# A chunked scan's attention products moved from GpSimd to VectorE, with C·B read from PSUM and the residual sum put last in the loop

## The chip, the cores and the metric

One core of a Trainium2 chip (trn2). The metric is the device time of the whole program in microseconds (us). A NeuronCore has five engines with a queue each, which meet through semaphores: TensorE (PE; its weight loads are PEld), VectorE (DVE), ScalarE (ACT), GpSimd (POOL) and SyncE (SP), which here issues the DMAs. Matmul results land in eight banks of PSUM; everything else is in SBUF.

## The reference

`x` is 16 images of 192 channels, 32 by 32 pixels, float32. Two blocks run on each image, each with a group norm ahead and a residual sum behind:

```
x = x + L0(_gn(x))      # in-projection, 3x3 depthwise convolution, silu, chunked scan, layer norm, gate, out-projection
x = x + L1(_gn(x))      # projection, selective scan with 16 states per channel, out-projection
```

The chunked scan of L0 goes over 1024 tokens in 8 chunks of 128, with 12 heads of 32 channels and a state of 32. For a chunk it is

```
att = einsum('bcihn,bcjhn->bcijh', Ch, Bh) * Lmat * dtc      # Lmat = exp(cumsum_i - cumsum_j), causal
y_intra = einsum('bcijh,bcjhp->bcihp', att, xc)
y_inter = Ch . exp(cumsum) . state before the chunk
state = state * exp(whole chunk's sum) + B . decay . x
y = layer_norm(y_intra + y_inter + D x) * z, then the out-projection
```

C·B, the first product of `att`, is the same for the 12 heads: it is one 128x128 matrix for a chunk.

## The kernel before, in words

A pass handles two images at once: the selective scan of L1 for image b, and all of L0 (with the first part of L1) for image b+1. There is a first pass with L0 alone (image 0), a last one with the end of L1 alone, and a loop over two passes in the middle. Each pass is cut into 48 slots. The order on each engine is the order of the code: every engine has a function `run` that walks the slots `s` and calls, in a slot, the parts of both images. The engines are tied by semaphores only (`wait_ge` and `then_inc`).

**L1's selective scan.** One unit per slot, 48 units of 128x512. ScalarE makes the decay (L955: `dec`, or `bank`), VectorE makes the input `wr` (L1234) and runs the scan into `hst` (L1247), GpSimd multiplies by C into `hc` (L754), and TensorE sums two units' `hc` with `sel` every even slot (L1284, `bank<-hc,sel`). In a slot VectorE does scan and `wr` after its parts of `first_block_soon` and ahead of `first_block_later`.

**L0's chunked scan.** `chunk_at(s, stage)` says which chunk c is at a stage: slot s = 14 + 2c + stage. A chunk takes two slots per step, and up to five chunks are under way at once. In slots of stage 0, 2, 4, 6, 8 ("even") and 1, 3, 5, 7, 9 ("odd"):

- stage 0: TensorE: `b_by_c` (C·B into bank 4, `B_CBT`, columns 0 to 127; in the trace `bank<-cs_,bs`), the first group of `rows` (L1368: four heads' cumulative sums spread over 128 rows), `transposed_x` (L1382, L1383).
- stage 1: TensorE: `from_state` (`bank<-state,cs_`, in front of it the wait for the state), `rows` 1, later in the slot `rows` 2. ScalarE: the exponentials of group 0 (L831, into `att`), the copy of x to `xtok` (L875), the copy of C·B to the SBUF tile `cbt` (L879). GpSimd: `scaled_x` (L701), then `attention` for heads 0 to 3 (L710: `att` times `cbt`, which is repeated for each head).
- stage 2: ScalarE: the exponentials of groups 1 and 2 (L831). GpSimd: `attention` for heads 4 to 11 (L710). TensorE: `own_state`. VectorE: `from_state` (L1088).
- stage 3: TensorE: `chunk_output`, first with `diagd`, then 12 matmuls of 128x32 that read `att`. VectorE: `carry_state` (L1082, L1083: the state times its decay, plus the bank).
- stage 4: VectorE: `chunk_output` (L1102, L1099 for the first chunk: the sum of y; L1105 to L1108: its statistics). GpSimd: `layer_rstd` (L715).
- stage 5: VectorE: `normalise` (L1112). TensorE: `transposed_y` into bank 4, columns 128 to 511 (L1430).
- stage 6: ScalarE: the bank copy to `yzt` with weight and bias of the norm (L861). TensorE: `gate`.
- stage 7: VectorE: `gate` (L1119: `yzt` times the gate's bank).
- stage 8: TensorE: `projected` (`bank<-ssd,wo`).
- stage 9: VectorE: `residual` (L1125, L1126).

All tiles of L0's scan (`att`, `xtok`, `xw`, `yint`, `y0`, `yzt`) are parts of one SBUF tensor named `ssd` in the trace. `att` and `cbt` have two copies each, for even and odd chunks. VectorE's order inside an odd slot is residual, state, norm, gate, scan, `wr`; inside an even slot it is `from_state`, sum of y with statistics, scan, `wr`. The helper `mm` puts most matmuls on L1284.

## Time and profile before

| | us |
|---|---|
| median of three runs | 4015.2 |
| the three runs | 4018.0, 3992.5, 4015.2 |
| the profiled execution | 3989.6 |
| its span, first to last instruction | 3987.8 |
| mean granted clock of TensorE | 0.89 of full speed |
| distance from one image to the next in the middle of the run | about 241 |

The distance between images is read from GpSimd's rows: the same product of two images starts at 2000.35 and 2241.76 us. Busy time and rows are of the profiled execution. A row gives an instruction's start and duration; in brackets stands how long its engine had been idle, and whose end released it. TensorE's rows overlap, since matmuls are pipelined.

### The profile page before, as it was taken

Reading aid. Unit: us, or ns where it says so; the run is one execution under the profiler, and the core shown is the slowest. Engines: PE = TensorE matmul, PEld = TensorE weight load, DVE = VectorE, ACT = ScalarE, POOL = GpSimd, SP = SyncE. Lnnn points to the kernel's source line nnn. Section 1 sums busy time; section 2 is a strip of 40 time slices with the busy share of each in tenths; the row PEclk is TensorE's granted clock in tenths of the full one; section 3 lists DMA queues with packets and bytes.
Section 4 is the critical chain, followed back from the end, with each engine's and each line's share of the span. In section 5 each row is a group of like instructions: output and inputs, shape, how many; then the busy total and the mean of one; then the engine's idle time right before and its main releaser. Section 6 shows DMA issues by size and latency. Waiting matters only on the chain. (4 is left out here: it accounts for less than half of the span.)

```text
span 3987.8 us, 62307 instructions
## 1 busy us (share of the span) xinstructions
PE 3274.6 (82%) x20256; PEld 1864.8 (47%) x20256; DVE 2674.3 (67%) x3855; ACT 1844.2 (46%) x4475; POOL 2035.9 (51%) x1363
## 2 busy tenths in 40 slices
PE   4778888887987978888887897978888888888875
PEld 2645446363453635436363463635536354463620
DVE  1346857678585776757678575775757668575798
ACT  1425454363544536444463534535454353544542
POOL 1325546364453745546365463745546364563755
PEclk8989989898998989989898998989989898998986
DMA  3032131312213132130422213132131312313122
GB/s 64 1 94 68 68 86 34 112 62 79 81 40 112 51 107 74 67 82 33 120 62 78 81 40 112 51 106 69 48 108 33 118 63 74 82 45 101 62 73 77
DMA packets 104179, 291.11 MB, mean 73 GB/s; under 512 B 25373, under 2 KB 27020, under 8 KB 103820
## 3 DMA queue, kind: packets, MB, share of 16 engines
q1 hardware_dynamic: 103820, 286.71, 23.8%
q8 instruction: 179, 2.93, 0.3%
q14 instruction: 180, 1.47, 0.1%
HBM read 181.84 MB, written 39.85 MB: 56 GB/s over the span
## 5 line engine op out<-in xcount | busy, mean ns | idle before, releaser
L754 POOL TENSOR_TENSOR hc<-hst,bcrep 128x512 f32<-128x512 f32 x768 | 1187.6, 1546 | 1227.8 <-DVE hst L1247 1199.8
L710 POOL TENSOR_TENSOR ssd<-ssd,cbt 128x512 f32<-128x512 f32 (+1 forms) x256 | 585.4, 2287 | 383.8 <-ACT ssd L831 364.2
L1234 DVE TENSOR_TENSOR wr<-durep,bcrep 128x512 f32<-128x512 f32 x768 | 644.4, 839 | 65.1 <-DMA bcrep<-bc_rows 65.1
L1284 PE MATMUL bank<-hc,sel 128*32 128x512 f32 x1536 | 474.6, 701 | 104.2 <-POOL hc L754 104.2
L955 ACT ACTIVATE bank<-durep,aneg 128x512 f32<-128x512 f32 x368 | 252.0, 690 | 514.0 <-DVE hst L1247 468.5
L831 ACT ACTIVATE ssd<-bank,ncs 128x128 f32<-128x128 f32 x1536 | 432.8, 401 | 74.6 <-PE bank L1284 72.5
L1284 PE MATMUL bank<-ssd 128*128 128x32 f32 (+1 forms) x3296 | 448.0, 288 | 7.4 <-POOL ssd L710 7.4
L1247 DVE TENSOR_TENSOR_SCAN hst<-dec,wr 128x512 f32<-128x512 f32 x256 | 358.2, 1399 | 135.6 <-ACT dec L955 63.0
L1284 PEld LDWEIGHTS bank<-ssd 128*128 128x128 f32 x3296 | 397.8, 193 | 15.1 <-POOL ssd L710 10.8
L1284 PE MATMUL bank<-xna,wt0a 128*128 128x128 f32 (+3 forms) x1088 | 320.1, 398 | 76.2 <-DVE xnb L1065 76.2
L861 ACT ACTIVATE ssd<-bank,nbc,nwc 128x128 f32<-128x128 f32 x384 | 147.8, 454 | 498.8 <-PE bank L1430 498.5
L1284 PE MATMUL bank<-ssd,wcv 64*32 64x512 f32 x5376 | 344.1, 591 | 0.0
L1247 DVE TENSOR_TENSOR_SCAN hst<-bank,carry,wr 128x512 f32<-128x512 f32 x240 | 306.9, 1279 | 29.4 <-issue 11.2
L955 ACT ACTIVATE dec<-durep,aneg 128x512 f32<-128x512 f32 x400 | 294.1, 740 | 7.1 <-DVE hst L1247 4.6
L1284 PE MATMUL bank<-xnb,wt0b 128*128 128x128 f32 (+3 forms) x1088 | 295.3, 374 | 0.0
L1284 PEld LDWEIGHTS bank<-xna,wt0a 128*128 128x128 f32 (+1 forms) x1088 | 183.1, 203 | 232.3 <-issue 195.5
L1368 PE MATMUL bank<-ident,csum 128*128 128x128 f32 x1536 | 257.3, 294 | 30.6 <-ACT ssd L831 30.6
L1368 PEld LDWEIGHTS bank<-ident,csum 128*128 128x128 f32 x1536 | 196.2, 149 | 89.4 <-ACT ssd L831 49.6
L1125 DVE TENSOR_TENSOR x1a<-bank,xa 128x128 f32<-128x128 f32 x128 | 37.1, 290 | 285.7 <-PE bank L1284 285.7
L1284 PEld LDWEIGHTS bank<-xnb,wt0b 128*128 128x128 f32 (+1 forms) x1088 | 178.7, 201 | 76.6 <-issue 76.6
L1247 DVE TENSOR_TENSOR_SCAN hst<-dec,carry,wr 128x512 f32<-128x512 f32 x144 | 209.2, 1453 | 6.9 <-issue 2.8
L1284 PE MATMUL bank<-ssd,wo 128*128 128x128 f32 (+1 forms) x1536 | 211.9, 280 | 1.2 <-DVE ssd L1119 1.0
(188 smaller groups left out, 5022.5 us busy)
## 6 DMA issues: line engine op xcount, KB each, us to landing
durep<-scratch SPq DMA_DIRECT2D x192, 512.0 KB, 3.8
bcrep<-bc_rows SPq DMA_DIRECT2D x128, 512.0 KB, 5.5
ssd<-stage SPq DMA_DIRECT2D x384, 140.4 KB, 2.9
ssd<-bcst SPq DMA_DIRECT2D x128, 74.4 KB, 2.1
xa<-in_x_dram SPq DMA_DIRECT2D x16, 512.0 KB, 5.3
scratch<-u SPq DMA_DIRECT2D x32, 256.0 KB, 2.0
scratch<-delta SPq DMA_DIRECT2D x32, 256.0 KB, 2.2
out_dram<-x1a SPq DMA_DIRECT2D x16, 512.0 KB, 5.1
```

The costliest lines, as they stand in the source:

```text
L710: nc.gpsimd.tensor_tensor(a, a, bc(cbt[:, c % 2, :].unsqueeze(1), [P, h1 - h0, Q]), ALU.mult).then_inc(att_ready.sem, 1)
L754: nc.gpsimd.tensor_tensor(hc[:, i % CRING, :], hst[:, i % HRING, :], bcrep[:, g, 1, :], ALU.mult).then_inc(hc_ready.sem, 1)
L831: ins = nc.scalar.activation(att[:, c % 2, h, :], bank[ROW_BANKS[r]][:, k * Q:(k + 1) * Q], ACT.Exp, bias=ncs[:, c, h:h + 1])
L861: ins = nc.scalar.activation(yzt[:, c % 2, m, :], bank[B_CBT][:, (m + 1) * Q:(m + 2) * Q], ACT.Identity, bias=nbc[:, m:m + 1], scale=nwc[: ...
L955: nc.scalar.activation(decay_of(i), durep[:, j % SLOTS_DU, 0, :], ACT.Exp, scale=aneg1[:, g * NB + k:g * NB + k + 1]).then_inc(decay_ready ...
L1125: nc.vector.tensor_tensor(x1a[par][:, t], bank[B_OUT][:, 0:Q], xa[:, t], ALU.add).then_inc(x1_ready.sem, 1)
L1234: nc.vector.tensor_tensor(wr[:, i % WRING, :], durep[:, j % SLOTS_DU, 1, :], bcrep[:, g, 0, :], ALU.mult).then_inc(w_made.sem, 1)
L1247: nc.vector.tensor_tensor_scan(hst[:, i % HRING, :], decay_of(i), wr[:, i % WRING, :], carry[:, g:g + 1] if hf else 0.0, ALU.mult, ALU.add ...
L1284: return nc.tensor.matmul(out, lhsT, rhs, start=start, stop=stop, skip_group_check=True)
L1368: nc.tensor.matmul(ps[:, k * Q:(k + 1) * Q], bc(csum[:, 0, c, h:h + 1], [P, P]), ident[:, :], start=(k == 0), stop=False, is_transpose=Tru ...
```

## The change

- The attention products are made by VectorE in one instruction for all 12 heads (1536 elements), reading C·B from bank 4 as it is; it stands at the end of the even slot (stage 2), in `first_block_later`. GpSimd's two products and ScalarE's copy to `cbt` go, and with them the tile and its semaphore.
- `b_by_c` moves from stage 0 to stage 2, ahead of the `rows` in the same even slot. Since bank 4 is shared, it waits for the products of the chunk before and for the bank copy of the chunk two before; `transposed_y` waits for the products too.
- ScalarE does the exponentials of group 1 ahead of the bank copy of stage 6, and those of group 2 behind it.
- VectorE's residual sum moves from the head of the odd slot to its end, behind scan and `wr`.

```diff
-            def attention(n, c, h0, h1):
-
-                pool.wait_ge(row_exp.sem, row_exp.at(n, NRB * c + h1 // HPB))
-                pool.wait_ge(cbt_copied.sem, cbt_copied.at(n, c + 1))
-                a = att[:, c % 2, h0:h1, :]
-                nc.gpsimd.tensor_tensor(a, a, bc(cbt[:, c % 2, :].unsqueeze(1), [P, h1 - h0, Q]),
-                                        ALU.mult).then_inc(att_ready.sem, 1)
...
-                    attention(n, c, 0, HPB)
-                c = chunk_at(s, 2)
-                if c >= 0:
-                    attention(n, c, HPB, NH)
...
+                c = chunk_at(s, 2)
+                if c >= 0:
+                    exp_rows(n, c, 1)
                 c = chunk_at(s, 6)
...
                 c = chunk_at(s, 2)
                 if c >= 0:
-                    exp_rows(n, c, 1)
                     exp_rows(n, c, 2)
...
-                    act.wait_ge(cb_ps.sem, cb_ps.at(n, c + 1))
-                    if c >= 2:
-                        act.wait_ge(att_ready.sem, att_ready.at(n, 2 * (c - 1)))
-                    nc.scalar.copy(cbt[:, c % 2, :], bank[B_CBT][:, 0:Q]).then_inc(cbt_copied.sem, 1)
...
+            def attention(n, c):
+
+                dve.wait_ge(row_exp.sem, row_exp.at(n, NRB * (c + 1)))
+                dve.wait_ge(cb_ps.sem, cb_ps.at(n, c + 1))
+                a = att[:, c % 2, :, :]
+                nc.vector.tensor_tensor(a, a, bc(bank[B_CBT][:, 0:Q].unsqueeze(1), [P, NH, Q]), ALU.mult).then_inc(att_ready.sem, 1)
...
-                c = chunk_at(s, 9)
-                if c >= 0:
-                    if c == 0 and again:
-
-                        dve.wait_ge(stored.sem, stored.at(n - 2, 32))
-                    residual(n, c, par)
                 c = chunk_at(s, 3)
...
+                c = chunk_at(s, 2)
+                if c >= 0:
+                    attention(n, c)
                 c = chunk_at(s, SSD_LAST)
+                if c >= 0:
+                    if c == 0 and again:
+
+                        dve.wait_ge(stored.sem, stored.at(n - 2, 32))
+                    residual(n, c, par)
...
                 if c >= 1:
-                    pe.wait_ge(cbt_copied.sem, cbt_copied.at(n, c))
-                if c >= 3:
-
-                    pe.wait_ge(yt_made.sem, yt_made.at(n, c - 2))
+                    pe.wait_ge(att_ready.sem, att_ready.at(n, c))
+                if c >= 2:
+
+                    pe.wait_ge(yt_made.sem, yt_made.at(n, c - 1))
                 mm(bank[B_CBT][:, 0:Q], bs[:, t], cs_[:, t], True, True).then_inc(cb_ps.sem, 1)
...
-                if c + 2 < NCH:
-                    pe.wait_ge(cbt_copied.sem, cbt_copied.at(n, c + 3))
-                else:
+                if c + 1 < NCH:
+                    pe.wait_ge(att_ready.sem, att_ready.at(n, c + 2))
+                if c >= 1:
                     pe.wait_ge(yt_made.sem, yt_made.at(n, c))
...
+                c = chunk_at(s, 2)
+                if c >= 0:
+                    b_by_c(n, c)
                 c = chunk_at(s, 0)
                 if c >= 0:
...
-                    b_by_c(n, c)
```

The order on VectorE in a chunk with all stages under way, before: from scan and `wr` of an even slot (L1247, L1234) through the odd slot to the sum of y (`x1a`, `x1b` are the residual, `state` the state, `ssd` L1112 the norm, L1119 the gate):

```order
L1234 TENSOR_TENSOR wr<-durep,bcrep 128x512 [waits scanned]
L1125 TENSOR_TENSOR x1a<-bank,xa 128x128 [waits o0_ps]
L1126 TENSOR_TENSOR x1b<-bank,xb 64x128
L1082 TENSOR_TENSOR state<-state,cexp 32x384 [waits state_ps]
L1083 TENSOR_TENSOR state<-state,bank 32x384 [waits dve_steps]
L1112 TENSOR_SCALAR ssd<-ssd,lmv,lrs 128x384 [waits lrs_ready]
L1119 TENSOR_TENSOR ssd<-ssd,bank 128x384 [waits z_ps,yt_made]
L1247 SCALAR_TENSOR_TENSOR hst<-dec,wr 128x512 [waits hc_ready,carried,w_made,decay_ready]
L1234 TENSOR_TENSOR wr<-durep,bcrep 128x512 [waits scanned]
L1088 TENSOR_TENSOR ssd<-bank,cexp 128x384 [waits inter_ps]
L1102 TENSOR_TENSOR ssd<-ssd,bank 128x384 [waits yint_ready,yt_ps,y_ps]
```

The same place now (`ssd` L1104 of 128x1536 is the attention product; the lines of the code have shifted):

```order
L1227 TENSOR_TENSOR wr<-durep,bcrep 128x512 [waits scanned]
L1104 TENSOR_TENSOR ssd<-ssd,bank 128x1536 [waits cb_ps,row_exp]
L1066 TENSOR_TENSOR state<-state,cexp 32x384 [waits state_ps]
L1067 TENSOR_TENSOR state<-state,bank 32x384 [waits dve_steps]
L1096 TENSOR_SCALAR ssd<-ssd,lmv,lrs 128x384 [waits lrs_ready]
L1110 TENSOR_TENSOR ssd<-ssd,bank 128x384 [waits z_ps,yt_made]
L1240 SCALAR_TENSOR_TENSOR hst<-dec,wr 128x512 [waits hc_ready,carried,w_made,decay_ready]
L1227 TENSOR_TENSOR wr<-durep,bcrep 128x512 [waits scanned]
L1116 TENSOR_TENSOR x1a<-bank,xa 128x128 [waits o0_ps]
L1117 TENSOR_TENSOR x1b<-bank,xb 64x128
L1072 TENSOR_TENSOR ssd<-bank,cexp 128x384 [waits inter_ps]
L1086 TENSOR_TENSOR ssd<-ssd,bank 128x384 [waits yint_ready,yt_ps,y_ps]
```

The product is new ahead of the state update; the residual, with its wait for the projection (`o0_ps`), went from ahead of the state update to behind `wr`.

The order on ScalarE in an even slot of such a chunk, before (L955 is the decay, L861 the bank copy, L831 the exponentials, four heads each):

```order
L955 ACTIVATE dec<-durep,aneg 128x512 [waits scanned,du_read0]
L861 ACTIVATE ssd<-bank,nbc,nwc 128x128 [waits o0_ps,yt_ps]
L861 ACTIVATE ssd<-bank,nbc,nwc 128x128 x2
L831 ACTIVATE ssd<-bank,ncs 128x128 [waits row_ps]
L831 ACTIVATE ssd<-bank,ncs 128x128 x3
L831 ACTIVATE ssd<-bank,ncs 128x128 [waits row_ps]
L831 ACTIVATE ssd<-bank,ncs 128x128 x3
```

And now (L939 is the decay, L817 the exponentials, L850 the bank copy):

```order
L939 ACTIVATE dec<-durep,aneg 128x512 [waits scanned,du_read0]
L817 ACTIVATE ssd<-bank,ncs 128x128 [waits row_ps]
L817 ACTIVATE ssd<-bank,ncs 128x128 x3
L850 ACTIVATE ssd<-bank,nbc,nwc 128x128 [waits o0_ps,yt_ps]
L850 ACTIVATE ssd<-bank,nbc,nwc 128x128 x2
L817 ACTIVATE ssd<-bank,ncs 128x128 [waits row_ps]
L817 ACTIVATE ssd<-bank,ncs 128x128 x3
```

One group of exponentials passed the bank copy, the other stayed behind it.

## Rows read from the trace of the kernel before

**Rows 1.** The page, busy time of the engines (share of the span), count

```profile
PE 3274.6 (82%) x20256; PEld 1864.8 (47%) x20256; DVE 2674.3 (67%) x3855; ACT 1844.2 (46%) x4475; POOL 2035.9 (51%) x1363
```

**Rows 2.** Stretches: us; busy PE, PEld, DVE, ACT, POOL; clock; DMA share, GB/s

```profile
2019.13:2030.79 11.66, 9.65 (x61) 6.76 (x62) 10.52 (x13) 8.53 (x25) 11.57 (x8) 1.00 0.06 25
2030.79:2042.70 11.91, 10.50 (x74) 8.26 (x74) 10.66 (x14) 8.96 (x25) 8.59 (x7) 1.00 0.16 45
2042.70:2056.37 13.67, 12.15 (x87) 9.62 (x87) 9.99 (x17) 6.54 (x22) 10.23 (x8) 1.00 0.14 40
...
2083.71:2097.52 13.81, 12.79 (x89) 9.97 (x89) 9.36 (x17) 5.98 (x20) 9.30 (x7) 1.00 0.00 1
```

**Rows 3.** Timeline of PE in one full chunk: start, us, instruction, idle before

```profile
2070.04 0.91 PE L1284 MATMUL bank<-state,cs_ 128*128 128x384 f32 x2 [1.29 <-DVE state L1083]
...
2076.80 0.49 PE L1284 MATMUL bank<-cs_,bs 128*128 128x128 f32 x2
...
2077.52 0.65 PE L1368 MATMUL bank<-ident,csum 128*128 128x128 f32 x4 [0.23 <-ACT ssd L831]
```

**Rows 4.** Timeline of DVE in the same chunk

```profile
2068.20 0.29 DVE L1125 TENSOR_TENSOR x1a<-bank,xa 128x128 f32<-128x128 f32 x1 [3.47 <-PE bank L1284]
...
2068.60 0.81 DVE L1082 TENSOR_TENSOR state<-state,cexp 32x384 f32<-32x384 f32 x1
2069.44 0.54 DVE L1083 TENSOR_TENSOR state<-state,bank 32x384 f32<-32x384 f32 x1
...
2070.75 0.54 DVE L1119 TENSOR_TENSOR ssd<-ssd,bank 128x384 f32<-128x384 f32 x1
...
2072.41 1.68 DVE L1234 TENSOR_TENSOR wr<-durep,bcrep 128x512 f32<-128x512 f32 x1
...
2074.91 0.56 DVE L1102 TENSOR_TENSOR ssd<-ssd,bank 128x384 f32<-128x384 f32 x1 [0.35 <-PE bank L1284]
...
2077.87 0.67 DVE L1234 TENSOR_TENSOR wr<-durep,bcrep 128x512 f32<-128x512 f32 x1
```

**Rows 5.** Waits: engine, line, whom it waited for: us, times, longest

```profile
PE bank L1284 <- DVE state L1083: 124.5, 94, 2.7
```

**Rows 6.** Groups by shape, the products on GpSimd: busy us, mean ns

```profile
L710 POOL TENSOR_TENSOR ssd<-ssd,cbt 128x1024 f32<-128x1024 f32 x128 | 314.3, 2455 | 364.5 <-ACT ssd L831 364.2
...
L710 POOL TENSOR_TENSOR ssd<-ssd,cbt 128x512 f32<-128x512 f32 x128 | 271.2, 2118 | 19.3 <-ACT cbt L879 19.3
```

**Rows 7.** Timeline of POOL in the same chunk

```profile
2070.58 2.97 POOL L710 TENSOR_TENSOR ssd<-ssd,cbt 128x512 f32<-128x512 f32 x1
```

**Rows 8.** Timeline around the second `state` matmul of the image

```profile
2026.83 2.79 DVE L1234 TENSOR_TENSOR wr<-durep,bcrep 128x512 f32<-128x512 f32 x1
...
2029.54 0.54 DVE L1082 TENSOR_TENSOR state<-state,cexp 32x384 f32<-32x384 f32 x1
...
2030.79 0.88 PE L1284 MATMUL bank<-state,cs_ 128*128 128x384 f32 x2 [2.02 <-DVE state L1083]
```

**Rows 9.** Groups by shape on DVE: busy us, mean ns, idle before

```profile
L1247 DVE TENSOR_TENSOR_SCAN hst<-bank,wr 128x512 f32<-128x512 f32 x128 | 156.1, 1219 | 56.8 <-ACT bank L955 53.1 <-issue 2.5
...
L1119 DVE TENSOR_TENSOR ssd<-ssd,bank 128x384 f32<-128x384 f32 x128 | 68.7, 537 | 0.0
...
L1125 DVE TENSOR_TENSOR x1a<-bank,xa 128x128 f32<-128x128 f32 x128 | 37.1, 290 | 285.7 <-PE bank L1284 285.7
```

**Rows 10.** Timeline of ACT in the same chunk: the bank copy

```profile
2075.28 1.16 ACT L861 ACTIVATE ssd<-bank,nbc,nwc 128x128 f32<-128x128 f32 x3 [4.90 <-PE bank L1430]
```

**Rows 11.** Timeline of the tail: the last chunks' output and norm

```profile
2108.47 2.87 PE L1284 MATMUL bank<-ssd 128*128 128x32 f32 x24 [0.25 <-POOL ssd L710]
...
2108.94 1.41 DVE L1112 TENSOR_SCALAR ssd<-ssd,lmv,lrs 128x384 f32<-128x384 f32 x1 [1.07 <-POOL lrs L715]
...
2118.22 0.55 PE L1430 MATMUL bank<-ident,ssd 128*128 128x128 f32 x3 [0.96 <-DVE ssd L1112]
```

**Rows 12.** Group on PE, the head rows' wait: busy us, mean ns, idle before

```profile
L1368 PE MATMUL bank<-ident,csum 128*128 128x128 f32 x1536 | 257.3, 294 | 30.6 <-ACT ssd L831 30.6
```

More of the change, by code:

```diff
@@ L249, in build @@
         wend = sb("wend", [P, NCH, NH])
-        cbt = sb("cbt", [P, 2, Q])
         state = sb("state", [P, DI])
@@ L343, in build @@
         cb_ps = sig("cb_ps", NCH)
-        cbt_copied = sig("cbt_copied", NCH)
         row_ps = sig("row_ps", NCH * NRB)
         row_exp = sig("row_exp", NCH * NRB)
-        att_ready = sig("att_ready", 2 * NCH)
+        att_ready = sig("att_ready", NCH)
         xw_ready = sig("xw_ready", NCH - 1)
@@ L1415, in chunk_output @@
                     mm(bank[B_XY][:, m * P:(m + 1) * P], xs[m][:, t], diagd[:, m, :], m == 0, False)
-                pe.wait_ge(att_ready.sem, att_ready.at(n, 2 * (c + 1)))
+                pe.wait_ge(att_ready.sem, att_ready.at(n, c + 1))
                 for h in range(NH):
```

## The prediction

> **What bounds the kernel now.** I read the page first, then the stretches between two fixed points, then the waits, then four engines' rows of one chunk. TensorE is the busiest engine by far: 3274.6 us of a span of 3987.8, against 2674.3 for VectorE and 2035.9 for GpSimd [rows 1]. That is a mean and decides nothing, so I looked at the scan over chunks of one image (slots 14 to 37) in the middle of the run. Its fixed points are the starts of the matmul that reads `state` in front of chunks 1 to 7. The six distances are 11.66, 11.91, 13.67, 13.67, 13.67 and 13.81 us, and TensorE is busy for 9.65, 10.50, 12.15, 12.15, 12.16 and 12.79 of them [rows 2] (the first three and the last; the two between read as the third). So 1.0 to 2.0 us of each chunk is TensorE idle, at a granted clock of 1.00.
>
> What ends that idle time stands in the chunk's rows. After the transposes of x TensorE waits 1.29 us, until VectorE's update of the state ends (2069.44 + 0.54); another 0.23 us it waits for ScalarE's exponentials [rows 3]. The rows of VectorE say why the update is late: VectorE sat idle for 3.47 us in front of the residual sum at 2068.20, which needs the output projection, the last work of TensorE before those transposes. Residual and state update stand in one queue, so the update (0.81 and 0.54 us) starts only when the projection is through, though its own input was there 3 us before [rows 4]. The wait table confirms this for the whole run: 124.5 us in 94 waits for that one instruction [rows 5].
>
> GpSimd is the second cause, and it rules the early chunks. It spends 271.2 + 314.3 us on the products that the change takes away [rows 6]. While one runs, a VectorE product of two SBUF tiles waits for its end: at 2072.41 `wr` took 1.68 us beside GpSimd's 2.97 us product (from 2070.58), and ended 0.5 us after it; at 2077.87, with GpSimd idle, it took 0.67 [rows 4, 7]. At 2026.83 it took 2.79 us, just ahead of a state update that TensorE waited 2.02 us for [rows 8].
>
> **The change, part by part.** It moves no DMA and nothing in the queues of SyncE.
>
> Residual last. The state update no longer stands behind the projection. In a full chunk (chunks 3 to 6) that ends the 1.29 us wait, if nothing else of VectorE is as late; that is the sum over the new chain below.
>
> The product on VectorE. One instruction of 1536 elements, one operand in PSUM. The trace has no such size. The nearest rows are the product of an SBUF tile with a PSUM bank: 128x384 in 537 ns, the sum of the same kind 128x128 in 290 ns [rows 9]. That is 0.965 ns per element and 0.166 us fixed: 0.166 + 1536 x 0.965 ns = 1.65 us, the value I take. Below it there is little: 1536 elements at that slope alone are 1.48 us. Above it, the slowest VectorE form near by is the scan, 1219 ns for 512 elements [rows 9], thus 2.38 ns per element and 3.66 us; with a wait for a GpSimd product of 1.27 us on top, 4.93 us.
>
> Whether it waits for GpSimd matters. Product and gate share one form (SBUF times PSUM), and the gate at 2070.75 began inside GpSimd's product and still took 0.54 us [rows 4, 7]; all 128 of them have a mean of 537 ns. So no wait, 1.65 us. The Trainium skill says the same from the other side (GPSIMD Engine Reference, Key points): GpSimd contends with VectorE instructions that have two SBUF inputs or run in a two-port mode. By that rule `wr` waits and the new product doesn't, and the trace agrees (1.68 against 0.54). The skill also has a rule that speaks against reading PSUM (VectorE: DVE Perf Modes, the TRN2 errata): a PSUM source costs 120 cycles fixed and an SBUF one 58. By it the product would be an estimated 1656 cycles at 0.96 GHz, 1.73 us. That makes the two chunks below that VectorE sets 0.08 us longer and the others not at all, some 2.5 us in the run.
>
> The new chain on VectorE. From the state update's end to TensorE's matmul 0.06 us; from that matmul (2070.04) to the sum of y (2074.91) 4.87; from there through statistics, scan and `wr` to 2078.54, 3.63; the new product 1.65; the update, without GpSimd beside it 0.54 + 0.54 with gaps, 1.11 [rows 3, 4, 8]. Sum 11.3 us per chunk. What the product waits for is there by then: in full chunks ScalarE's last exponentials now follow the bank copy (2075.28 + 1.16 + some 1.1 = 2077.6) and C·B ends at 2077.3, both ahead of 2078.54 [rows 10, 3]. Queued behind the product are the state update and all of the odd slot, and TensorE waits for the update; that is in the chain.
>
> Which is longer, chunk by chunk. Distances 1 and 2: chain 11.3 against TensorE's 9.65 and 10.50; the chain sets the pace: 11.66 + 11.91 - 2 x 11.3 = 1.0 us. Distances 3 to 5: TensorE's 12.15 is longer, 3 x (13.67 - 12.15) = 4.6 us. Distance 6: 13.81 - 12.79 = 1.0. Together 6.6 us.
>
> The exponentials moved. The second group runs in ScalarE's 4.90 us of idle time instead of behind it [rows 10]; that ends the 0.23 us wait, already in the 12.15. The copy of C·B (0.27 us on ScalarE) goes; ScalarE is idle beside it: nothing.
>
> C·B two steps later. As many matmuls per slot; it now waits for the bank copy (end 2076.44), which is 0.36 us before TensorE comes to it anyway, at 2076.80 [rows 3, 10]. Only the last one is extra, in a slot that had none: +0.42 us, its 0.49 less the overlap with the next. In the first image TensorE has no units of the other scan to sum ahead of it, and the wait shows, some 0.5 us per chunk (my estimate from the same two rows).
>
> The tail (chunk 7's output). A wait of 0.25 us for GpSimd's product goes and one of 0.96 us for the norm, which stood behind a residual [rows 11]; 0.25 + 0.96 - 0.42 = 0.8. The norm after it waited 1.07 us for a power that GpSimd did behind its product [rows 11]; I count half. Tail: 1.3 us.
>
> Sum: 6.6 + 1.3 = 7.9 us in each of 15 images, 119; the first image 7.9 less 6 x 0.5 and the early chunks, some 6. 125 us in all. The profiled execution took 3989.6 us (span 3987.8 and 1.8 around it): 3865. The runs' median lies 0.6% above it, their fastest at 3992.5, so a run may come out anywhere from 3865 to 3890; I name 3875.
>
> **Rivals.**
>
> B, the port: the product waits for GpSimd's product in progress, 1.27 us more. For it: every SBUF-SBUF form does so. Against: the gate doesn't. Chain 11.3 + 1.27 = 12.6: the early pair loses 1.6 us, the full chunks gain 3 x 1.1, the last 1.0, the tail 0.8: 3.5 us (3 x 1.1 + 1.0 + 0.8 - 1.6) x 16 = 56, 3935.
>
> C, slower: the product is priced above the point where the new chain outlasts the old distances. The six distances are 78.4 us, with the tail's 0.8 they are 79.2, and the chain is 9.67 + p: 79.2 / 6 = 13.2, so p = 3.5 us. At 4.93 us (rate of the scan plus the wait) the chain is 14.6, six of them 87.6, 8.4 us lost per image: 3990 + 16 x 8.4 = 4125. For it: only the scan's row. Against: three rows of the nearer form.
>
> D, no gain: the wait is only exchanged. The product comes ahead of the state update and needs all three groups of exponentials; if they or the rate put it at 3.5 us behind `wr` in place of 1.65, the point above is met: 3990. For it: the copy waits for TensorE's transposes, one chain more. Against: 0.9 us of slack at 2078.54.
>
> E, more: the early chunks too fall to TensorE's time, and in the tail VectorE's gain carries into the next stage; TensorE's two waits of the chunks go in all (124.5 and 30.6 us) [rows 5, 12] and the tail's 1.3 x 16 = 21 with them: 176 us, 3814, or somewhat less, up to 3830.
>
> **How the numbers follow.** Chances: forecast 0.68 (own range 3835 to 3910), B 0.12, C 0.04, D 0.06, E 0.10. The range reaches from E's edge to B with the runs' 0.6% on it: 3818 to 3955. Over 1% faster (1% is about what a measurement tells from no change; 3950 or less): forecast, E and most of B, 0.87. Within 1%: D and some of B and C, 0.09. Slower 0.04.
>
> **What would show it.** Right: 128 VectorE products near 1.65 us; the `state` matmuls 12.2 us apart in full chunks and 11.3 in the first; TensorE's wait for the state update near zero in full chunks and 1 to 2 us in the two early ones; `wr` near 0.7 us throughout; the residual without idle time ahead. Wrong: a product over 2.5 us, or distances still over 13; a new wait of TensorE for the product or for the bank copy; a product that lasts longer where GpSimd works.

## The result, and the profile after

The changed kernel takes 3838.6 us (median of four runs, 3832.4 to 3840.1), against 4003.9 us for the kernel before in the same session (3992.4 to 4018.0). The ratio is 0.958, 95% interval 0.954 to 0.963. A second session of five runs gave 3843.3 us against 3990.9, ratio 0.962 (0.960 to 0.964). The forecast was 3875 us in a range of 3818 to 3955; the measured 3838.6 is 36 us below the 3875 and inside the range. The profiled execution of after took 3839.4 us with a span of 3837.7, at a mean granted clock of 0.89 as before, so the profiled executions lie 150 us apart where 125 were forecast. One run of all that follow was slow, e2's second (9435 us at a granted clock of 0.33), and e2's median leaves it out.

The page of after, busy time of the engines, beside [rows 1]:

```profile
PE 3214.6 (84%) x20256; PEld 1841.5 (48%) x20256; DVE 2655.5 (69%) x3983; ACT 1829.5 (48%) x4347; POOL 1498.1 (39%) x1107
```

GpSimd is relieved of 538 us. VectorE, which took over the products (223.7 us), is busy for 19 us less than before: its other instructions got shorter by more than that, `wr` alone by 122 us. TensorE's busy time falls by 60 us with the same count of matmuls. Of that, 26 us stand in the distances 3 to 6 (783.5 to 757.8 us over all images, at a granted clock of 1.00 in both), which says that "busy" held something there that was no work; more on that below. Another 29 us stand in the convolution's stretch, where the clock isn't full, and are not explained by it.

The stretches between `state` matmuls of one image in the middle of the run, columns as in [rows 2] (the first, second, third, fourth and last distance; the one left out reads as the fourth):

```profile
1953.28:1964.81 11.53, 9.65 (x62) 6.78 (x62) 8.51 (x14) 7.86 (x23) 6.32 (x5) 1.00 0.07 21
1964.81:1975.89 11.08, 10.28 (x74) 8.23 (x74) 8.39 (x15) 8.54 (x24) 3.76 (x3) 1.00 0.08 30
1975.89:1987.66 11.77, 11.77 (x86) 9.66 (x87) 9.79 (x17) 5.74 (x19) 4.66 (x4) 1.00 0.12 46
1987.66:1999.34 11.68, 11.68 (x89) 9.58 (x87) 9.36 (x18) 6.26 (x20) 4.90 (x4) 1.00 0.41 143
...
2011.01:2023.54 12.53, 12.53 (x90) 9.95 (x89) 10.42 (x19) 6.26 (x18) 5.09 (x4) 1.00 0.00 1
```

From the third distance on TensorE has no idle time at all; the first two still hold 1.9 and 0.8 us of it. TensorE's rows of a full chunk, answering to [rows 3], show both old waits gone (more rows of before stand further down):

```profile
2005.99 0.49 PE L1277 MATMUL bank<-cs_,bs 128*128 128x128 f32 x2
2006.32 0.60 PE L1361 MATMUL bank<-ident,csum 128*128 128x128 f32 x4
2006.76 0.38 PE L1277 MATMUL bank<-maskneg,identb 128*128 128x512 bf16 x1
...
2010.90 0.27 PE L1376 MATMUL bank<-ident,bs 128*128 128x128 f32 x1
2011.01 0.81 PE L1277 MATMUL bank<-state,cs_ 128*128 128x384 f32 x2
2011.66 0.60 PE L1361 MATMUL bank<-ident,csum 128*128 128x128 f32 x4
```

VectorE's rows of the same chunk, answering to [rows 4]. The product stands right behind `wr`, the state update right behind the product, the residual behind the next `wr` with no idle time:

```profile
2007.07 0.67 DVE L1227 TENSOR_TENSOR wr<-durep,bcrep 128x512 f32<-128x512 f32 x1
2007.65 1.75 DVE L1104 TENSOR_TENSOR ssd<-ssd,bank 128x1536 f32<-128x1536 f32 x1
2009.31 0.54 DVE L1066 TENSOR_TENSOR state<-state,cexp 32x384 f32<-32x384 f32 x1
2009.89 0.54 DVE L1067 TENSOR_TENSOR state<-state,bank 32x384 f32<-32x384 f32 x1
...
2012.99 0.27 DVE L1116 TENSOR_TENSOR x1a<-bank,xa 128x128 f32<-128x128 f32 x1
```

The update ends at 2010.43, 0.58 us ahead of the matmul that reads it. The waits of the whole run, answering to [rows 5] and [rows 12]:

```profile
PE bank L1277 <- DVE state L1067: 42.7, 32, 2.7
PE bank L1361 <- ACT ssd L817: 22.4, 17, 1.5
PE bank L1277 <- DVE state L1064: 9.9, 16, 1.3
```

The wait for the state update fell from 124.5 us (94 times) to 42.7 (32 times, two per image). The wait for ScalarE's exponentials that is left (22.4 us of 30.6) stands ahead of the first `state` matmul, once per image, and not in the full chunks. The wait for the first chunk's copy of the state, 16 times 0.20 us before, has grown to 9.9 us. VectorE's groups by shape, beside [rows 9]. First `wr` in the kernel before, then after:

```profile
L1234 DVE TENSOR_TENSOR wr<-durep,bcrep 128x512 f32<-128x512 f32 x768 | 644.4, 839 | 65.1 <-DMA bcrep<-bc_rows 65.1
```

```profile
L1227 DVE TENSOR_TENSOR wr<-durep,bcrep 128x512 f32<-128x512 f32 x768 | 522.0, 680 | 47.0 <-DMA bcrep<-bc_rows 47.0
...
L1104 DVE TENSOR_TENSOR ssd<-ssd,bank 128x1536 f32<-128x1536 f32 x128 | 223.7, 1748 | 53.1 <-PE bank L1277 34.5 <-ACT ssd L817 18.6
...
L1116 DVE TENSOR_TENSOR x1a<-bank,xa 128x128 f32<-128x128 f32 x128 | 35.3, 276 | 2.9 <-PE bank L1277 2.7
```

`wr`, untouched by the change, is 0.16 us shorter as a mean. GpSimd's products are what made it long: in e6 below, the kernel before without them, its mean is 693 ns. The residual's idle time fell from 285.7 us to 2.9.

Where the time went, over all 16 images. The program is cut at the same instructions in both traces (start of the `csum` copy on VectorE, the seven `state` matmuls, the second instruction of the last residual, the next `csum` copy), and each distance summed:

| stretch | before | after | difference | forecast |
|---|---|---|---|---|
| `csum` to first `state` matmul | 328.5 | 338.3 | +9.8 | 0 |
| distances 1 and 2 | 382.3 | 359.4 | -22.9 | -16 |
| distances 3 to 5 | 654.9 | 561.2 | -93.8 | -74 |
| distance 6 | 220.7 | 199.4 | -21.3 | -16 |
| last `state` matmul to next `csum` | 2293.3 | 2271.6 | -21.7 | -21 |
| all, with the program's start | 3987.8 | 3837.7 | -150.1 | -125 |

(The forecast's 2 us less for the first image are in its last line only.)

Two lines of this table hold something besides the change, the granted clock. The first distance of before took 11.67 us in 12 of the 14 middle images (11.46 in one of them) and 14.20 in two, where the clock stood at 0.76:

```profile
1058.65:1072.85 14.20, 13.07 (x62) 8.86 (x62) 10.99 (x13) 7.09 (x23) 12.65 (x9) 0.76 0.16 65
```

After has no such image. The distances 3 to 6 stood at 1.00 in both kernels, so their lines are clean.

### The profile page after: what moved, and what is told of

It is laid out like the page before. It is cut to its first block and busy times, and to the rows that moved or that the text cites. A ratio compares the mean times of both kernels' runs of the same rounds, so it can differ in the third digit from the quotient of the medians.

```text
span 3837.7 us, 61535 instructions
## 1 busy us (share of the span) xinstructions
PE 3214.6 (84%) x20256; PEld 1841.5 (48%) x20256; DVE 2655.5 (69%) x3983; ACT 1829.5 (48%) x4347; POOL 1498.1 (39%) x1107
## 5 line engine op out<-in xcount | busy, mean ns | idle before, releaser
L1227 DVE TENSOR_TENSOR wr<-durep,bcrep 128x512 f32<-128x512 f32 x768 | 522.0, 680 | 47.0 <-DMA bcrep<-bc_rows 47.0
L1277 PE MATMUL bank<-hc,sel 128*32 128x512 f32 x1536 | 466.1, 690 | 102.9 <-POOL hc L740 101.3
L817 ACT ACTIVATE ssd<-bank,ncs 128x128 f32<-128x128 f32 x1536 | 440.4, 380 | 112.9 <-PE bank L1277 110.3
L939 ACT ACTIVATE bank<-durep,aneg 128x512 f32<-128x512 f32 x368 | 251.9, 689 | 504.6 <-DVE hst L1240 464.8
L1240 DVE TENSOR_TENSOR_SCAN hst<-dec,wr 128x512 f32<-128x512 f32 x256 | 341.3, 1333 | 141.4 <-ACT dec L939 98.3
L699 POOL TENSOR_TENSOR ssd<-ssd,wend 128x384 f32<-128x384 f32 x112 | 157.5, 1406 | 372.9 <-ACT ssd L863 372.3
L939 ACT ACTIVATE dec<-durep,aneg 128x512 f32<-128x512 f32 x400 | 290.5, 730 | 7.1 <-DVE hst L1240 4.6
L850 ACT ACTIVATE ssd<-bank,nbc,nwc 128x128 f32<-128x128 f32 x384 | 147.8, 454 | 302.9 <-PE bank L1423 302.9
L1104 DVE TENSOR_TENSOR ssd<-ssd,bank 128x1536 f32<-128x1536 f32 x128 | 223.7, 1748 | 53.1 <-PE bank L1277 34.5
L705 POOL TENSOR_TENSOR lrs<-lve,neghalf 128x1 f32<-128x1 f32 x128 | 75.5, 590 | 384.6 <-DVE lve L1092 381.7
```

Of the source, the lines that this page charges most:

```text
L699: nc.gpsimd.tensor_tensor(xw[:, c % 2, :].rearrange("p (h d) -> p h d", d=HD), xtok[:, c % 2, 0:DI].rearrange("p (h d) -> p h d", d=HD), b ...
L705: nc.gpsimd.tensor_tensor(lrs[:, c % 2:c % 2 + 1], lve[:, c % 2:c % 2 + 1], neghalf[:, 0:1], ALU.pow).then_inc(lrs_ready.sem, 1)
L817: ins = nc.scalar.activation(att[:, c % 2, h, :], bank[ROW_BANKS[r]][:, k * Q:(k + 1) * Q], ACT.Exp, bias=ncs[:, c, h:h + 1])
L850: ins = nc.scalar.activation(yzt[:, c % 2, m, :], bank[B_CBT][:, (m + 1) * Q:(m + 2) * Q], ACT.Identity, bias=nbc[:, m:m + 1], scale=nwc[: ...
L939: nc.scalar.activation(decay_of(i), durep[:, j % SLOTS_DU, 0, :], ACT.Exp, scale=aneg1[:, g * NB + k:g * NB + k + 1]).then_inc(decay_ready ...
L1104: nc.vector.tensor_tensor(a, a, bc(bank[B_CBT][:, 0:Q].unsqueeze(1), [P, NH, Q]), ALU.mult).then_inc(att_ready.sem, 1)
```

## The experiments

The runs were made in three sessions (e1 to e4; e5 to e8; e9 to e12); each ratio is against the kernel before of the same session. Below, "six distances" are those between `state` matmuls, as a mean over the 14 middle images, worked out from the matmuls' starts. For before they are 12.02, 11.91, 13.66, 13.67, 13.66, 13.82, and for after 11.52, 11.08, 11.77, 11.67, 11.67, 12.53: 78.7 and 70.2 us per image. A mean of the first two can hold images at a lower granted clock; where it does, the text says so.

**e1: the kernel before, with the residual last and nothing else.**

```diff
-                c = chunk_at(s, 9)
-                if c >= 0:
...
-                    residual(n, c, par)
                 c = chunk_at(s, 3)
...
                 c = chunk_at(s, SSD_LAST)
+                if c >= 0:
...
+                    residual(n, c, par)
```

> The kernel before with one edit: the residual sum goes behind scan and wr. Products stay on GpSimd. My theory (the state update stood behind the projection in VectorE's queue; that alone is the 1.3 us wait of full chunks): the distance between state matmuls in full chunks falls from 13.67 to about 12.1 us, the early two stay at 11.7 and 11.9, 6 us per image, about 3895 us for a run of 3990. Rival (GpSimd's products beside VectorE are what makes the update late): full chunks stay above 13.2 us, over 3960 us.

Measured: 3902.0 us (3896.8 to 3909.3), ratio 0.975 (0.972 to 0.977). The stretches of one image, first, second and a full chunk:

```profile
1986.10:1997.78 11.68, 9.65 (x62) 6.78 (x62) 10.12 (x13) 8.54 (x25) 11.18 (x8) 1.00 0.03 12
1997.78:2009.68 11.90, 10.50 (x75) 8.26 (x75) 10.66 (x14) 8.94 (x25) 8.59 (x7) 1.00 0.16 45
...
2021.89:2034.01 12.12, 11.89 (x88) 9.53 (x87) 11.78 (x17) 6.42 (x21) 9.07 (x7) 1.00 0.36 130
```

The full chunks fall from 13.67 to 12.12 with GpSimd's products still in place; the early ones don't move in this image. Over the run the first is longer as a mean (12.74), because six of the 14 images took 14.20 us at a granted clock of 0.76; the other eight took 11.67 (one of them 11.47), as before. So it is the queue behind the residual that held the full chunks, not GpSimd, and this part alone is worth 100 us. Of these the traces ascribe only the distances, 79 us, to it: the stretch from the last `state` matmul to the last residual grew from 30.05 to 32.92 us per image, and the convolution's behind it fell from 110.5 to 107.5. What of these two is the edit and what the clock isn't separated.

**e2: after, with the residual back at the head of the odd slot** (the diff of e1 backwards).

> The changed kernel with one edit undone: the residual sum is back at the head of the odd slot. My theory: TensorE's wait for the state update is back in full chunks, distance about 13.1 us (13.67 less 0.39 for the exponentials and 0.27 for a state product that no longer waits for GpSimd), early two as in the changed kernel (11.5 and 11.1), 5 to 6 us per image, about 3925 us. Rival (relief of GpSimd did it): full chunks under 12.2 us, about 3850.

Measured: 3906.2 us (3905.7 to 3909.6), ratio 0.977 (0.973 to 0.980). Six distances 11.52, 11.08, 13.02, 12.96, 12.96, 13.82. VectorE in a full chunk:

```profile
2025.53 1.75 DVE L1104 TENSOR_TENSOR ssd<-ssd,bank 128x1536 f32<-128x1536 f32 x1
2028.64 0.29 DVE L1116 TENSOR_TENSOR x1a<-bank,xa 128x128 f32<-128x128 f32 x1 [1.36 <-PE bank L1278]
```

The product is done early, the residual waits for the projection again and the state update behind it is late: TensorE waits for it for 109.1 us in the run. The early distances are exactly those of after, since no residual stands in them. Moving the products alone doesn't free the full chunks; moving the residual alone doesn't free the early ones.

**e6: the kernel before, with GpSimd's products cut to one column.** The attention products are left out (the output lacks them); waits and signals stay.

```diff
-                a = att[:, c % 2, h0:h1, :]
-                nc.gpsimd.tensor_tensor(a, a, bc(cbt[:, c % 2, :].unsqueeze(1), [P, h1 - h0, Q]),
+                a = att[:, c % 2, h0, 0:1]
+                nc.gpsimd.tensor_tensor(a, a, cbt[:, c % 2, 0:1],
```

> The kernel before with the products left out: GpSimd multiplies one column where it did 512 or 1024 elements, so the attention isn't scaled by C.B; queues, waits and order stay. It prices GpSimd's products as such. My theory: early distances fall by about 1 us each (to 10.5 and 10.9), full chunks only to 13.4 us, since the residual is still ahead of the state update; some 3 us per image, about 3945 us. Rival (GpSimd's contention is the main thing): full chunks under 12.5 us, under 3900 us.

Measured: 3886.7 us (3871.2 to 3898.9), ratio 0.972 (0.969 to 0.976). The first, second and a full distance of one image:

```profile
1968.38:1977.96 9.58, 9.58 (x61) 6.74 (x61) 6.56 (x13) 6.47 (x22) 6.03 (x6) 1.00 0.04 15
1977.96:1988.56 10.60, 10.37 (x75) 8.37 (x75) 8.26 (x14) 10.00 (x24) 6.01 (x7) 1.00 0.13 49
...
2001.93:2015.33 13.40, 12.15 (x86) 9.62 (x86) 8.30 (x17) 6.35 (x22) 6.04 (x7) 1.00 0.46 156
```

This is e1's mirror: full chunks stay at 13.4 us, while the early two fall to 9.58 and 10.60, TensorE's own time or nearly so (9.58 and 10.37 busy). The gain is well above the expectation's 3945, because three places gain and not two: 2.4 + 1.3 us in the early distances, 0.8 over the other four, and 2.1 in the stretch from the last `state` matmul to the last residual (30.05 to 27.97): 6.6 us per image, some 106 in the run. Some 1.2 us of the 6.6 is the clock, which stood below 1.00 in before: against its images at 1.00 (11.67 for the first distance, 29.18 from the last `state` matmul to the last residual) the gain is 5.4. GpSimd's products cost the early chunks and the tail more than the forecast had seen.

**e3 and e12: after, with ScalarE's order undone**, and **e9: e1 with ScalarE's order of the change added.** The edit of e3; e9 makes it the other way:

```diff
-                c = chunk_at(s, 2)
-                if c >= 0:
-                    exp_rows(n, c, 1)
                 c = chunk_at(s, 6)
...
                 if c >= 0:
+                    exp_rows(n, c, 1)
                     exp_rows(n, c, 2)
```

> The changed kernel with ScalarE's order undone: the exponentials of group 1 behind the bank copy again. My theory: TensorE waits for them again (0.23 us and the refill, 0.4 us) and the VectorE product gets its last group 1.1 us later, which its slack of 0.9 us nearly covers: full chunks 12.0 to 12.3 us against 11.67, some 2 us per image, about 3870 us. Rival (ScalarE has slack in any order): 3840, distance 11.67.

> The kernel before with two of the change's parts alone: residual sum last, and the exponentials of group 1 ahead of the bank copy; the products stay on GpSimd. With the residual alone (run e1) the full chunks took 12.1 to 12.2 us, the early two 12.74 and 11.92, the whole 3902. Theory: the full chunks fall to 11.7 us, since GpSimd's products set nothing there, and the early two stay at 12.7 and 11.9, since those are GpSimd's. If a microsecond of a chunk is a microsecond of the run, that is 3 x 0.45 x 16 = 22 us and some 3880. Rival, the gain comes back elsewhere: in the stage of the convolution, whose length goes with the granted clock, so that the run stays at 3900 while the chunks are shorter.

e9 measured 3862.2 us (3852.5 to 3870.3), ratio 0.968 (0.965 to 0.970), where e1 has 0.975: ScalarE's order is worth some 30 us there, taken across two sessions. Its full chunks took 11.7 us as after's do, with the products still on GpSimd. The early distances are shorter than e1's as well (12.20 and 11.57), which the theory hadn't expected. For the first that is only the clock: 11.67 us in the images at 1.00 as in e1, but three at 0.76 and not six. For the second it is real (11.90 to 11.55 at 1.00).

e3 measured 3835.8 us (3835.3 to 3843.9), ratio 0.959 (0.957 to 0.962), that is, no loss against after at all. Yet its full chunks took 12.12 us against 11.67. The expectation of a repeat, in one session with after:

> Run e3 once more (the changed kernel with the exponentials of group 1 behind the bank copy). Full chunks 12.1 us, 1.6 us more per image over the chunks. Theory, given back: the time is that of the changed kernel again, within 5 us, and the stage of the convolution some 1.5 to 2.3 us shorter per image (106.7 against 109.0 before), at a higher granted clock. Rival, chance: the equal times of the first pair were luck, and this one is 15 to 25 us slower than the changed kernel.

> The changed kernel once more, beside its version with ScalarE's order undone, so that the two have the same chip and the same minutes. 3839 within 8 us. In its profile the full chunks stay at 11.67 us; the stage of the convolution (109.0 us per image in the first profile) tells how far that one moves from one execution to another.

e12 measured 3837.7 us (3832.0 to 3841.7) and after again (e11) 3843.3 (3837.9 to 3846.4): not chance. The chunks of e12 are longer by 1.6 us per image (71.9 against 70.2), and it is not slower. What pays for that stands in the stretch behind the chunks, from the last residual to the next `csum` copy, where the convolution runs: 106.9 us as a mean in e12 and 106.7 in e3, against 109.0 in both profiles of after. The mean granted clock there was 0.85 in e12 and e3, and 0.83 and 0.84 in the two of after. The stretch of one image, after first and then e3:

```profile
2053.53:2160.80 107.27, 88.63 (x545) 34.63 (x546) 66.71 (x93) 40.89 (x78) 39.22 (x27) 0.86 0.37 111
```

```profile
2050.98:2153.57 102.59, 85.44 (x545) 33.05 (x546) 66.80 (x92) 40.80 (x78) 39.41 (x27) 0.87 0.39 116
```

The work is the same; TensorE's matmuls are busy for 3.2 us longer in after, at a lower granted clock. What makes this stage's clock differ between two kernels that differ only in the chunks isn't shown by any run.

**e10: e5 (below) with ScalarE's order undone**, to see whether this gift comes with the order itself.

> The kernel of run e5 (product behind the state update) with ScalarE's order undone: the exponentials of group 1 behind the bank copy again. The pair e5 and e10 repeats the pair after and e3 at a shorter distance in the early chunks. Theory: full chunks 12.1 us against 11.67, thus 22 us more in the chunks; if that reaches the end, 3784 + 22 = 3806. Rival, given back: the time stays within 8 us of 3784, and the stage of the convolution is shorter by some 1.5 us per image at a higher granted clock.

Measured: 3808.5 us (3800.2 to 3814.8), 24 us above e5's 3784.2 of another session; ratio 0.953 (0.951 to 0.956) against e5's 0.948, whose interval (0.944 to 0.952) just overlaps. Full chunks 12.11 us. Its stretch of the convolution is 108.0 us, e5's 107.5: no gift this time, and the 0.45 us per full chunk reach the end. So ScalarE's part is worth some 22 to 30 us in two of three pairs, both taken across sessions, and nothing in the kernel as changed.

**e4: after, with C·B read from an SBUF tile** that ScalarE copies from the bank.

```diff
+                    act.wait_ge(cb_ps.sem, cb_ps.at(n, c + 1))
+                    nc.scalar.copy(cbt[:, c % 2, :], bank[B_CBT][:, 0:Q]).then_inc(cbt_copied.sem, 1)
...
-                nc.vector.tensor_tensor(a, a, bc(bank[B_CBT][:, 0:Q].unsqueeze(1), [P, NH, Q]), ALU.mult)
+                nc.vector.tensor_tensor(a, a, bc(cbt[:, c % 2, :].unsqueeze(1), [P, NH, Q]), ALU.mult)
```

> The changed kernel with C.B copied to an SBUF tile by ScalarE (0.27 us, behind the last exponentials) and the VectorE product reading that tile: two SBUF operands. If a product of two SBUF operands waits for GpSimd's hc product, its mean is 1.7 plus up to 1.3 us, about 2.9, every chunk's distance is 12.5 to 12.8 us, about 3925 us. If reading PSUM is what costs (0.1 us over my 1.65), the product is shorter here, 1.6 to 1.7 us, and the time is that of the changed kernel, 3835 to 3845.

Measured: 3919.8 us (3917.8 to 3939.7), ratio 0.981 (0.978 to 0.985): half of the gain is gone. GpSimd and VectorE in a full chunk:

```profile
2044.03 1.63 POOL L742 TENSOR_TENSOR hc<-hst,bcrep 128x512 f32<-128x512 f32 x1 [0.81 <-DVE hst L1246]
```

```profile
2044.45 2.83 DVE L1110 TENSOR_TENSOR ssd<-ssd,cbt 128x1536 f32<-128x1536 f32 x1
```

With two SBUF operands the product takes 2.83 us beside `hc` and, at its shortest in the run, 1.74, which is what the PSUM form takes everywhere. `hc` had 1.21 us left when the product began (2044.03 + 1.63 - 2044.45); 2.83 less 1.21 is 1.62, so it waited for `hc`'s end and then ran. That holds over the run: 104 of the 128 products of e4 began inside an `hc` that had 0.06 to 1.22 us left, and each is as long as that rest and 1.61 to 1.70 us more; the 24 others took 1.74 to 1.76. In after the product at 2007.65 took 1.75, and all 128 lie between 1.739 and 1.756, most of them begun inside an `hc` too. The early distances, which VectorE's chain sets, grew to 12.64 and 13.83 as a mean. The second is 12.17 us in the images at a clock of 1.00, 1.1 us above after's 11.09 as the product's 2.83 is above 1.75; it is 13.82 at 0.88 and 15.5 at 0.67. So what the early chunks lose is the wait for `hc` and, as a mean, the clock. The copy has a small share: the product waited 61.3 us in the run for it, but 51 of these stand ahead of the first `state` matmul, in a stretch that is only 0.3 us per image longer than in after.

**e7: after, with the product cut to one column.** The attention product is left out.

> The changed kernel with the VectorE product left out (one column in place of 1536 elements, so the attention isn't scaled by C.B). It prices the product on VectorE's path. My theory: early distances fall by the product's 1.7 us until TensorE's own time stops them, to about 10.0 and 10.4 us, full chunks stay at 11.67 (slack), about 3800 us. Rival (VectorE's chain also sets the full chunks): they fall to about 10 us, under 3740 us.

Measured: 3780.1 us (3773.2 to 3789.3), ratio 0.944 (0.941 to 0.947). Six distances 10.64, 10.50, 11.77, 11.67, 11.67, 12.53. The full chunks don't change by 0.01 us: there the product's 1.7 us is free. The early ones do, by 1.5 us together: there VectorE is the bound. In the profiles, 50 us apart, these two distances give 24 us; another 21 stand in the convolution's stretch (107.4 us as a mean against 109.0), which the product doesn't touch.

**e5: after, with the product behind the state update** in the odd slot, in place of at the end of the even one.

```diff
                 if 0 <= c < NCH - 1:
                     carry_state(n, c, step)
+                if c >= 0:
+                    attention(n, c)
...
-                c = chunk_at(s, 2)
-                if c >= 0:
-                    attention(n, c)
```

> The changed kernel with the VectorE product moved behind the state update (from the end of the even slot to the odd slot, right behind carry_state). My theory (the early distances are set by the chain statistics, scan, wr, product, state update on VectorE; the full ones by TensorE's own back-to-back time): the first two distances fall from 11.5 and 11.1 to about 10.0 and 10.4 us, full chunks stay at 11.67, TensorE doesn't wait for the product; 2.3 us per image, about 3800 us. Rival (all distances are TensorE's or ScalarE's by now): no distance moves, 3835 to 3845.

Measured: 3784.2 us (3777.2 to 3808.0), ratio 0.948 (0.944 to 0.952), which beats both kernels and is within noise of e7, where there is no product at all. TensorE waits for the state and not for the product (the product's reader comes later), so the product is taken out of the early chunks' chain. Of the 62 us between the profiles of after and e5, 32 stand in the first two distances (10.16 and 10.51 as a mean), 8 in the stretch ahead of them, and 22 in the convolution's stretch; whether the edit has a hand in the last isn't shown, and in e8 below, with the same chunks, they are missing. The first two distances of one image, and what is left of the wait there:

```profile
1927.77:1938.40 10.63, 9.65 (x61) 6.77 (x62) 9.28 (x14) 7.34 (x21) 5.46 (x5) 1.00 0.03 12
1938.40:1948.90 10.50, 10.29 (x75) 8.24 (x75) 9.26 (x15) 8.83 (x24) 3.74 (x3) 1.00 0.14 51
```

```profile
1936.05 1.62 DVE L1066 TENSOR_TENSOR state<-state,cexp 32x384 f32<-32x384 f32 x1
```

```profile
1938.40 0.88 PE L1276 MATMUL bank<-state,cs_ 128*128 128x384 f32 x2 [0.98 <-DVE state L1067]
```

The wait that is left stands in every other image only; in the ones between, the first distance is TensorE's own 9.58 us. At 0.98 us it is nearly what the first half of the update (two SBUF operands) takes above its 0.54 us: it stretched to 1.62 with GpSimd at work, as `wr` did in [rows 4] (1.62 less 0.54 is 1.08).

**e8: e5, and C·B of chunk 0 made at stage 0 again.**

```diff
                 c = chunk_at(s, 2)
-                if c >= 0:
+                if c >= 1:
                     b_by_c(n, c)
...
                         pe.wait_ge(conv_done.sem, conv_done.at(n, XM))
+                        b_by_c(n, c)
```

> As the kernel with the product behind the state update, and C.B of chunk 0 alone back in its old slot (stage 0). The changed kernel's first product waits 2.6 us for that matmul, and the stretch up to the first state matmul is 0.6 us longer than before. My theory: that stretch is 0.6 us shorter again, 10 us in the run on top of the other kernel, about 3790 us; both together the fastest version. Rival: with the product behind the state update the first state matmul no longer depends on C.B, so nothing is added.

Measured: 3791.3 us (3777.6 to 3804.4), ratio 0.947 (0.943 to 0.951), no difference from e5 that this measurement can tell. The stretch from `csum` to the first `state` matmul did fall, from 20.99 us as a mean to 20.35; the 10 us that this makes drown in the convolution's stretch, 109.0 here and 107.5 in e5.

## Why the prediction was right, and where it was off

**The two causes and their places: right.** e1 and e6 separate them cleanly. The residual's queue holds the full chunks (13.67 to 12.12 by that part alone), GpSimd's products the early ones (11.67 and 11.90 to 9.58 and 10.60 without them, at a clock of 1.00).

**Full chunks, forecast -1.52 us each, measured -1.9 to -2.0.** This is the largest error, 20 of the 25 us by which the profiled executions miss the forecast. The step that failed is "TensorE's 12.15 is longer": I took TensorE's busy time for its work. Between the starts of the B transpose and of the `state` matmul lay 1.56 us before (2068.48 to 2070.04, the wait of [rows 3] between them) and lie 0.11 now: 1.45 gained for a row of 1.29. Between C·B and the head rows lay 0.72 (2076.80 to 2077.52) and now 0.33: 0.39 for a row of 0.23. Both waits cost 0.16 us more than their idle time, which the busy time held. The matmuls behind each wait are slower too, as these rows of before show:

```profile
2063.84 0.65 PE L1368 MATMUL bank<-ident,csum 128*128 128x128 f32 x4 [0.23 <-ACT ssd L831]
2064.33 0.38 PE L1284 MATMUL bank<-maskneg,identb 128*128 128x512 bf16 x1
...
2068.48 0.27 PE L1383 MATMUL bank<-ident,bs 128*128 128x128 f32 x1
2070.04 0.91 PE L1284 MATMUL bank<-state,cs_ 128*128 128x384 f32 x2 [1.29 <-DVE state L1083]
2070.79 0.60 PE L1368 MATMUL bank<-ident,csum 128*128 128x128 f32 x4
```

From the `state` matmul to the next start it is 0.75 us here and 0.65 in after (2011.01 to 2011.66), from the head rows to the next start 0.49 and 0.44 (2006.32 to 2006.76). With these the account closes: 1.45 + 0.39 + 0.10 + 0.05 = 1.99 us, the whole of 13.67 less 11.67. So a wait of 1.29 us cost 1.55, and one of 0.23 cost 0.44. e3 shows the second alone: with just the 0.23 us wait back, the distance is 12.12 and not 11.90. The Trainium skill (TensorE: Matmul & The Clock Gate, Step-by-step: what each phase is for, and Single matmul latency) explains the direction: a matmul on its own pays for its way through the array, and a following one hides it. Its fixed 398 cycles for a single bf16 matmul at 2.4 GHz would be an estimated 0.17 us; the trace's 0.16 us for float32 agrees, and the 0.05 to 0.10 behind the wait come on top.

**Early chunks, forecast -1.0 us for the two, measured -1.3 as a mean of 14 images, and -1.0 in the images of before at full clock.** The first distance goes from 11.67 to 11.53 there and the second from 11.90 to 11.09; the other 0.3 us of the mean are the two images of before at 0.76. The chain was forecast at 11.3 us, twice 22.6, and the two distances are 11.52 and 11.08, 22.6. That the sum is met so closely is luck, as two errors cancel. Its parts in the first: 4.87 us from the `state` matmul to the sum of y (1953.28 to 1958.15), 3.41 from there to the product (forecast 3.63), 1.66 to the next start, 1.6 for the update up to the matmul, which ran at 0.86 us and not 0.54 in its first half. In the second they are 4.84, 3.41, 1.66 and 1.17. So the way from the sum of y to the product was priced 0.22 us too long in both, and the update some 0.4 us too short in the first.

**Distance 6, forecast -1.0, measured -1.3:** the same hidden part of a wait, 0.26 us.

**The product, forecast 1.65 us and no wait for GpSimd: right.** Its row is 1.748 us, but the next instruction starts 1.66 us after it (2007.65 to 2009.31), since VectorE's rows overlap. Rival B falls by the 128 rows of after, which are all as long whether `hc` runs or not, and e4 shows the form that does wait. By the Trainium skill's rule cited in the forecast (VectorE: DVE Perf Modes, the TRN2 errata) the PSUM source has twice the fixed cost; its estimated 1.73 us is near the row, while e4's SBUF form at its shortest is as long, 1.744. Here PSUM as a source cost nothing that the rows show.

**The first image, forecast 2 us less than the others: wrong, but small.** The wait for the bank copy was priced at 0.5 us per chunk; in the whole run TensorE waits 4.1 us for that copy against 3.4 before, and the first image's full chunks fall by 2.0 us as the others' do (13.41 to 11.42). Its second distance falls by more, 13.58 to 10.30, but the one of before stood at a clock of 0.87. The forecast also has a slip of its own here: 7.9 less 6 x 0.5 is 4.9 and not 6, 1 us of the 125.

**C·B two steps later, forecast nothing ahead of the tail: wrong by +0.6 us per image.** What I missed is chunk 0. Its C·B now stands behind a unit's sum of the other scan, and VectorE's queue has the product ahead of the state's first copy:

```profile
1951.01 1.75 DVE L1104 TENSOR_TENSOR ssd<-ssd,bank 128x1536 f32<-128x1536 f32 x1 [2.56 <-PE bank L1277]
1952.68 0.54 DVE L1064 COPY state<-bank 32x384 f32<-32x384 f32 x1
```

```profile
1953.28 0.91 PE L1277 MATMUL bank<-state,cs_ 128*128 128x384 f32 x2 [0.57 <-DVE state L1064]
```

That wait was 0.20 us before. I had named what is queued behind the product only for the update, not for the first chunk's copy.

**Tail, forecast -1.3 us, measured -1.4 with the stretch behind it (21.7 us over 16 images): the agreement is luck.** From the last `state` matmul to the last residual it is 30.05 us before and 29.98 after as a mean. But before ran most of its tails at a granted clock of 0.94. At 1.00, where three of its 14 middle images stood and all of after's, it is 29.18 before and 29.98 after: 0.8 us longer, where 1.3 less were forecast. Two parts make this up. The products away from GpSimd give 1.0 to 1.2 us (29.18 to 28.19 in e2 and to 27.97 in e6, both at 1.00); the residual at the end of its slot takes 1.8 (28.19 in e2 to 29.98). The forecast had the residual's move as a gain here, the norm's 0.96 us wait. The residual is itself the mark that ends this stretch, so how much of the 1.8 us reaches the end of the run isn't shown. The gain of the table's line stands in the next stretch, 110.51 to 109.02, which goes with the clock and differed by 2 us between kernels with the same tail.

**Rivals.** C and D are out: the product keeps its price, and its chain ends 0.58 us early. E was half right: TensorE does run without a gap in the full chunks, at 11.67, but the early chunks stayed with VectorE, and 3839 lies between E's edge of 3830 and the forecast.

## What to carry to other kernels

A state update that the busiest engine reads must not stand in a queue behind an instruction that needs that engine's own last result; move the waiting instruction behind it before making anything faster, and put new work behind the update too, as e5 shows (another 54 us by the medians of two sessions, of which the traces ascribe 40 to it). The same work costs nothing where the busiest engine sets the pace and its full length where it doesn't, so price it stretch by stretch. And take a wait's price from starts to starts, not from the idle column alone.

## What the runs showed of the hardware

- **A wait of TensorE costs more than its idle row**: 1.55 us for a row of 1.29, 0.44 for one of 0.23 and, in e3 and e12 against after, 0.45 us of distance for a row of 0.23. Of that, 0.16 us each is the part of the last matmul that the next one hides when nothing waits, the rest is a slower start behind the wait. It is found in the busy time, which fell by 26 us in the distances 3 to 6 with the same matmuls.
- **The granted clock reaches into the chunks**: the first distance of before, e1 and e9 took 11.67 us at 1.00 and 14.20 at 0.76, in two, six and three of 14 images. After has no image at 0.76, and what decides it no run shows. A mean over images mixes the two.
- **VectorE's product of SBUF by PSUM ran beside GpSimd at full rate; the same product with both operands in SBUF waited for the end of GpSimd's instruction** (1.75 against 2.83 us, 1.21 of it wait). The Trainium skill (GPSIMD Engine Reference, Key points) names the two-input contention. The rows agree, and here the wait lasted until the end of GpSimd's instruction, in 104 of e4's products.
- **The convolution's stretch is not of one length in one kernel.** Two neighbouring images of e5's profile, from the last residual to the next `csum` copy:

```profile
1793.52:1906.44 112.92, 92.55 (x545) 35.81 (x546) 66.31 (x92) 40.88 (x78) 39.41 (x27) 0.82 0.36 106
2026.54:2129.53 102.99, 85.60 (x545) 32.88 (x546) 66.55 (x93) 40.79 (x78) 39.35 (x27) 0.87 0.39 115
```

The same 545 matmuls are busy for 92.6 us at a granted clock of 0.82 and for 85.6 at 0.87; the clock there moves between its two levels (1.2 and 2.4 GHz), and the other engines' busy times are the same. Of these two, the one with more time at the lower level is the longer. Ten microseconds an image are as much as this whole change gains per image, and a gain of 1.6 us per image in the chunks was seen to vanish in it (after against e3), and one of 1.3 to arrive in full (e5 against e10). Whether some placing of the chunks' work steers it stays open.
